# Mixture-of-experts rows that carry their weight, and gathers that add by DMA

## The reference, cut to what matters

```python
x = x + attn_a(layernorm(x))
x = x + ffn(layernorm(x))
x = x + attn_b(layernorm(x))
x = x + ffn(layernorm(x))

def ffn(x):                       # E = 16 experts, K = 2 choices, D = H = 128
    probs = softmax(xf @ router_w)
    w, idx = top_k(probs, K)
    ...                           # rank of each choice in its expert; keep = rank < capacity
    w = where(keep, w, 0.0)
    xe = x_pad[dispatch]          # rows sorted by expert
    hidden = silu(xe @ gate_w) * (xe @ up_w)
    out = (hidden @ down_w) * wbuf[:, :, None]
    combined = zeros.at[dispatch].add(out)
    return combined
```

## Time and profile before

| | us |
|---|---|
| three timed runs, median | 1406.74 |
| lowest and highest | 1403.67 and 1412.88 |
| profiled execution: its span | 1555.5 |
| TensorE busy in it | 1331.6 (86%) |
| VectorE busy | 1056.7 (68%) |
| GpSimd busy | 833.1 (54%) |
| ScalarE busy | 759.3 (49%) |

### The profile page before, as it was taken

One profiled execution on the slowest core, in us unless ns is written; L12 is line 12 of the kernel. 1 busy time (PEld: TensorE's weight loads), 2 busy tenths in 40 slices (PEclk: granted clock), 3 DMA queues, 4 the chain that ended last, 5 costly groups with the idle time before them and its releaser, 6 DMA issues.

```text
span 1555.5 us, 28624 instructions
## 1 busy us (share of the span) xinstructions
PE 1331.6 (86%) x8534; PEld 822.4 (53%) x8534; DVE 1056.7 (68%) x4590; ACT 759.3 (49%) x1901; POOL 833.1 (54%) x1246
## 2 busy tenths in 40 slices
PE   3999998978996989999999999999999999767400
PEld 1566655547885955444444444444455588656400
DVE  2899998883643477888778788787798546433422
ACT  2444444424544666666556566555566455333200
POOL 3247776675323133466666567755555345435576
PEclk9999998987998988999889799887699899988755
DMA  6755312013444410000000000020001134444432
GB/s 171 244 171 188 115 38 69 25 52 111 157 151 135 137 31 15 15 21 28 25 25 28 18 25 28 27 77 23 23 18 42 34 122 153 132 129 138 145 79 73
DMA packets 119785, 125.82 MB, mean 81 GB/s; under 512 B 15568, under 2 KB 109904, under 8 KB 119632
## 3 DMA queue, kind: packets, MB, share of 16 engines
q1 hardware_dynamic: 103248, 90.42, 18.3%
q0 software_dynamic: 16384, 33.59, 7.5%
HBM read 50.15 MB, written 73.79 MB: 80 GB/s over the span
## 4 chain that ended last, share of the span: by engine, by line
PE 68%; DVE 9%; issue 6%; another core or an unknown queue 5%; POOL 5%; ACT 4%; DMA 0%; ACTq 0%; POOLq 0%; DVEq 0%
PE pair L1897 27%; PE pair L1823 8%; PE pair L1834 4%; POOL vmyg L563 4%; PE pair L1685 4%; PE bank L1709 3%; DVE pT L1126 2%; PE pair L1812 2%; PE bank L1630 2%; DVE pT L1401 2%; PE bank L1925 1%; PE bank L1624 1%; PE bank L1951 1%; PE pair L1674 1%
## 5 line engine op out<-in xcount | busy, mean ns | idle before, releaser
L1897 PE MATMUL pair<-kT,apart 32*128 32x512 f32 x2048 | 500.4, 733 | 8.0 <-DVE smax L1401 6.5
L1401 DVE CUSTOM_DVE_ANT_0 pT<-pair,pT 128x256 f32<-128x256 f32 x1024 | 385.4, 417 | 128.5 <-ACT pT L924 110.1
L924 ACT ACTIVATE pT<-pair 128x256 f32<-128x256 f32 x1024 | 327.1, 395 | 257.1 <-PE pair L1897 229.2
L1897 PEld LDWEIGHTS pair<-kT,apart 32*128 32x128 f32 x2048 | 198.5, 208 | 155.4 <-DVE smax L1401 97.8
L563 POOL DMA_INDIRECT vmyg<-ybufA,slg x128 | 123.2, 962 | 149.8 <-DVE smax L1401 67.3
L1293 DVE TENSOR_TENSOR hid<-sg,pair 128x512 f32<-128x512 f32 x96 | 65.9, 686 | 197.6 <-ACT sg L850 171.2
L1823 PE MATMUL pair<-xeT,unit_w 128*128 128x256 f32 x768 | 195.6, 400 | 0.8 <-issue 0.8
L563 POOL DMA_INDIRECT vmyg<-ybufB,slg x128 | 122.7, 958 | 91.9 <-DVE smax L1401 47.6
L1126 DVE TENSOR_TENSOR pT<-pair,causal 128x512 f32<-128x512 f32 x256 | 159.5, 681 | 12.5 <-PE pair L1685 12.3
L1834 PE MATMUL pair<-unit_w,hid 128*128 128x128 f32 x768 | 110.7, 291 | 61.9 <-DVE ye L1301 61.6
L508 POOL DMA_INDIRECT dispB<-xnf,sli x128 | 127.4, 996 | 63.7 <-issue 36.2
(11 more groups left out here) (231 smaller groups left out, 2008.0 us busy)
## 6 DMA issues: line engine op xcount, KB each, us to landing
dispB<-zeros SPq DMA_DIRECT2D x16, 1408.0 KB
apart<-dispA SPq DMA_DIRECT2D x96, 128.0 KB
ybufA<-ye SPq DMA_DIRECT2D x48, 256.0 KB
apart<-dispB SPq DMA_DIRECT2D x96, 128.0 KB
ybufB<-ye SPq DMA_DIRECT2D x48, 256.0 KB
dispA<-zeros SPq DMA_DIRECT2D x33, 128.0 KB
xs<-in_x SPq DMA_DIRECT2D x16, 256.0 KB, 3.2
out<-xs SPq DMA_DIRECT2D x15, 256.0 KB
```

Source lines behind the costliest of these rows:

```text
L924: act.activation(rel[n % RING][:, q, :], pair[n % RING][:, q, HALF:SEQ], ACT.Relu).then_inc(s["relu_done"], 1)
L1401: dve.tensor_tensor_reduce(out=rel[n % RING][:, q, :], in0=pair[n % RING][:, q, 0:HALF], in1=rel[n % RING][:, q, :], scale=1.0, scalar=LOW ...
L1897: pe.matmul(pair[n % RING][:, q, :], apart[h][at, j, t * P:(t + 1) * P], kTs[h][at, HALF:], start=True, stop=True).then_inc(s["bsc_done"], 1)
```

## The change

A row that is sent now has 132 columns (528 bytes; `RW`): the 128 features, the weight in column 128, and three zeros. As a token's two choices have different weights, each tile has a copy for each choice: `rows` holds both, `xnf` is the first of them, and `twin` on ScalarE makes the second. `places` writes the weights there, and `wts` is gone. `y_copy` becomes a product of the result with column 128 of the group's rows, so the rows must stay in their tile until then: `load` of group g + 4 waits for `y_ready` of group g, and stands behind the store of g in SyncE's order. The gathers add straight into `xs` (`compute_op=ALU.add`), all those of a batch's first choice before those of its second; `yg`, `indices` and all of VectorE's additions are gone. Those who waited for the additions wait for the landing of the gathers of the second choice. The gathers that follow expert stages 2 and 3 are issued in two runs of eight batches, the second choice of a batch behind the first choice of the next.

```diff
+RW = D + 4
...
-        dispA = nc.dram_tensor("dispA", [DUMMY + UR, D], F32).ap()
+        dispA = nc.dram_tensor("dispA", [DUMMY + UR, RW], F32).ap()
...
-        xnf = [sb(f"xnf{r}", [P, TB, D]) for r in range(NF)]
+        rows = [sb(f"rows{r}", [P, TB, K, RW]) for r in range(NF)]
+        xnf = [t[:, :, 0, 0:D] for t in rows]
...
-        xe = [[apart[h][:, r, :].rearrange("p (j d) -> p j d", d=D) for r in range(NX)] for h in range(2)]
+        xe = [[turns[h][:, r * GT * RW:(r + 1) * GT * RW].rearrange("p (j d) -> p j d", d=RW) for r in range(NX)] for h in range(2)]
...
             def load(seg, g):
                 r = g % NX
                 if g >= NX:
-                    sp.wait_ge(s["xe_tp"], seg * GRP + g - NX + 1)
+                    sp.wait_ge(s["y_ready"], seg * GRP + g - NX + 2)
...
-                for g in range(GRP - 1):
+                for g in range(GRP - 3):
+                    store(g)
                     if g + NX < GRP:
                         load(seg, g + NX)
-                    if g >= 2:
-                        store(g - 2)
...
                     pool.wait_ge(s["slots_ready"], g + 1)
+                    pool.wait_ge(s["twin"], g + 1)
...
-                            in_=xnf[g % NF][:, j, :], in_offset=None, bounds_check=DUMMY - 1, oob_is_err=False,
+                            in_=rows[g % NF][:, j, k, :], in_offset=None, bounds_check=DUMMY - 1, oob_is_err=False,
...
-                pool.tensor_tensor(wts[:, cols].rearrange("p (t k) -> p t k", k=K), topw[:, :, :], keep[:, :, :], ALU.mult)
+                pool.tensor_tensor(rows[g % NF][:, :, :, D], topw[:, :, :], keep[:, :, :], ALU.mult)
...
+            def fetch(g, k, tiles=range(TB)):
+
+                b = g % B
+                if k == 0 and 0 in tiles:
+
+                    pool.wait_ge(s["tb"], SLOTS_AT[g // HALFB])
                     settle(pool)
+                if k and 0 in tiles:
+
+                    pool.wait_ge(s[f"first{g % 2}"], 16 * TB * (g // 2 + 1))
+                for j in tiles:
+                    at = (b * TB + j) * K + k
+                    done = "got_end" if k and (g, j) == (2 * B - 1, TB - 1) else f"{('first', 'second')[k]}{g % 2}"
                     pool.indirect_dma_start(
+                        out=xs[:, b * TB + j, :], out_offset=None, in_=ybuf[second(g)],
+                        in_offset=bass.IndirectOffsetOnAxis(ap=slots[:, at:at + 1], axis=0), compute_op=ALU.add,
+                    ).then_inc(s[done], 16)
...
-            stored(2)
-            fetch(B, 0)
-            fetch(B + 1, 1)
-            for b in range(2, B):
-                if b == HALFB:
-                    stored(3)
-                fetch(B + b, b % 2, end=range(K * (TB - 1), K * TB) if b == B - 1 else ())
+            for seg in (2, 3):
+                stored(seg)
+                at = B + FIRST[seg]
+                fetch(at, 0)
+                for n in range(1, HALFB):
+                    fetch(at + n, 0)
+                    fetch(at + n - 1, 1)
+                fetch(at + HALFB - 1, 1)
...
+            def twin(n):
+
+                act.wait_ge(s["ffn_xn_ready"], n + 1)
+                act.activation(rows[n % NF][:, :, 1, 0:D], xnf[n % NF], ACT.Copy).then_inc(s["twin"], 1)
...
-                    dve.tensor_copy(ye[h][:, :, :].rearrange("p j d -> p (j d)"), bank[7][:, :]).then_inc(s["y_ready"], 1)
+                    dve.tensor_tensor(ye[h][:, :, :], bank[7].rearrange("p (j d) -> p j d", j=GT),
+                                      xe[seg % 2][g % NX][:, :, D:D + 1].to_broadcast([P, GT, D]), ALU.mult).then_inc(s["y_ready"], 1)
...
-                    if fetch and n in (18, 19):
-                        add_first(b + 2, h, ((0, 1), (2, 3))[n - 18])
-                    if fetch and n in (20, 21):
-                        add_second(b + 2, h, ((0, 1), (2, 3))[n - 20])
                     if fetch and n == 22:
-                        dve.wait_ge(s["combined"], b + 3)
+                        dve.wait_ge(s[f"second{h}"], 16 * TB * (b // 2 + 2))
```

More of the change, by code:

```diff
@@ L190, in build @@
         tails = sb("tails", [1, E], I32)
-        apart = [sb(f"apart{h}", [P, GH, SEQ]) for h in range(2)]
-        whose = sb("whose", [P, NT * K, E])
-        xe = [[apart[h][:, r, :].rearrange("p (j d) -> p j d", d=D) for r in range(NX)] for h in range(2)]
+        turns = [sb(f"turns{h}", [P, NX * GT * RW]) for h in range(2)]
+        apart = [turns[h][:, 0:GH * SEQ].rearrange("p (j t) -> p j t", j=GH) for h in range(2)]
+        whose = sb("whose", [P, HALFB * TB * K, E])
+        xe = [[turns[h][:, r * GT * RW:(r + 1) * GT * RW].rearrange("p (j d) -> p j d", d=RW) for r in range(NX)] for h in range(2)]
         xeT = [sb(f"xeT{h}", [P, GT, D]) for h in range(2)]
@@ L245, in build @@
         block = ctx.enter_context(nc.Block())
+        SLOTS_AT = (28, 34, 51, 68)
         def tiles_of(b):
@@ L463, in _ @@
             pool.memset(ohsum[:, :], 0.0)
-            pool.memset(vmyg[:, :], 0.0).then_inc(s["vm_zero"], 1)
+            for r in range(NF):
+                pool.memset(rows[r][:, :, :, D:RW], 0.0)
+            pool.memset(vm[:, :, :], 0.0).then_inc(s["vm_zero"], 1)
             pool.memset(m8f[:, :], -1.0)
@@ L656, in _ @@
             stored(0)
-            fetch(0, 0)
-            fetch(1, 1)
+            for k in range(K):
+                fetch(0, k)
+                fetch(1, k)
             def selected_rows(b):
@@ L829, in attention_a @@
                     apply_norm(b + 2, b + 2, xna, "att", int(last), b + 2)
+                if last:
+                    twin(b - 1)
             apply_norm(0, 0, xna, "att", 0, 0)
@@ L875, in chain_a @@
                     turned(B - 1, "ffn", xfT)
+                    twin(B - 1)
                 if g == 5:
@@ L946, in body @@
                         context_x(b - 1)
+                    if before and n == 25:
+                        twin(b - 2 + B)
                     if before and n == 26:
@@ L974, in pieces @@
                     turned(2 * B - 2, "ffn", xfT)
+                    twin(2 * B - 2)
                 if g == 5:
@@ L983, in pieces @@
                     turned(2 * B - 1, "ffn", xfT)
+                    twin(2 * B - 1)
                 if g == 14:
@@ L1309, in experts @@
                 y_copy(G - 1)
-            def indices(b, h):
-                dve.tensor_copy(slg[h][:, :], slots[:, bass.ds(b * TB * K, TB * K)]).then_inc(s["slg_ready"], 1)
-            def add_choice(b, h, k, done, tiles=range(TB)):
-                for j in tiles:
-                    xb = xs[:, b * TB + j, :]
-                    last = dve.scalar_tensor_tensor(out=xb, in0=yg[h][:, K * j + k, :],
-                                                    scalar=wts[:, bass.ds((b * TB + j) * K + k, 1)], in1=xb,
-                                                    op0=ALU.mult, op1=ALU.add)
-                if TB - 1 in tiles:
-                    last.then_inc(done, 1)
-            def add_first(b, h, tiles=range(TB)):
-                if 0 in tiles:
-                    dve.wait_ge(s[f"got{h}"], (b // 2 + 1) * 16 * TB * K)
-                add_choice(b, h, 0, s["comb0"], tiles)
-            def add_second(b, h, tiles=range(TB)):
-                if 0 in tiles:
-                    dve.wait_ge(s["comb0"], b + 1)
-                add_choice(b, h, 1, s["combined"], tiles)
             def chain_a(g):
@@ L1370, in chain_a @@
                 if g == 15:
-                    indices(0, 0)
-                    indices(1, 1)
                     dve.wait_ge(s["w_in2"], 16 * 11)
@@ L1466, in body @@
                         residual(b - 2)
-                    if fetch and n == 1:
-                        indices(b + 2, h)
                     if b == MID + 2 and n == 29:
@@ L1811, in turn_x @@
                     for j in range(GT):
-                        last = pe.transpose(bank[2][:, j * P:(j + 1) * P], xe[seg % 2][r][:, j, :], ident[:, :])
+                        last = pe.transpose(bank[2][:, j * P:(j + 1) * P], xe[seg % 2][r][:, j, 0:D], ident[:, :])
                     last.then_inc(s["xe_tp"], 1)
```

80 lines of the change are left out of this document (16 added, 64 removed).

## The result

The changed kernel takes 1642.58 us (median of four runs, 1637.09 to 1654.80) where the kernel before takes 1405.88 beside it: a ratio of 1.1674, with a 95% interval of 1.163 to 1.1719. The sign was forecast, the size was not: 1498 us with a range up to 1555. A ratio leaves out runs that were over 1.5% slower than their kernel's fastest, so it isn't quite the quotient of the two medians.

The account below looks back on a forecast made before the run. It took TensorE to bound attention B and undisturbed expert stages, with gather issue on GpSimd in the tail. Loads +82, clock +12, additions -5, gathers +4, end -2 made +91 on 1406.7: 1498 us, range 1445 to 1555.

Parts of the forecast that it names:

- loads: idleness of TensorE in the stages: Expert stages: tiles refilled only after the result, so late loads stall TensorE; +82 us (60 to 100).
- clock in the stages: Expert stages: TensorE's granted clock falls after idle stretches; +12 us, between nothing and +37.
- attention B: VectorE's additions removed there, 34 us of its work but little of it time; -5 us, between 0 and -34.
- Undisturbed groups: Expert stages: 3.055 us a group at full clock, so four stages take some 310 to 330 us undisturbed.
- faster: Rival: stages at the profiled stage 3's 5.2 us a group, loads nearly in time, only additions count; 1375 us, chance 0.07.
- The loop: Expert stages, transposition to that four groups on: 14.76 us plus stalls against 12.22; stall 1.27 us, group 4.3 us.
- The gathers' price: Tail: a gather that adds by DMA costs 0.06 us more, +4 us; bounds 0 and 0.5 us each (32 us).
- dear gathers: Rival: gathers at 1.75 us each lengthen the tail by 32 us and outlast stage 3; 1537 us, chance 0.2.
- The signs: Timeline: load behind each store, TensorE idle over 1 us per transposition, stores 4.3 us apart, batches about 42, gathers at 1.25.
- Odd rows: Rival: 528-byte rows not starting at multiples of 512 bytes land after 3.2 us; 24 us more, 1522 us, chance 0.07.
- twin: ScalarE, 32 copies of 128x512 at some 0.7 us, needed half a batch later: 0, or 22 us without that cover.
- product: Expert stages, `y_copy`: the product costs what the copy did, 681 ns against 685.

Follow-up runs that it names:

- the two kinds of batch: Changed kernel, attention B gathers in one run, selected_rows behind the normalized rows: 1589.32 us, 1.1278; batches 38.3 us without a wait at pair 23, 48.4 with one.
- the last kernel: Changed kernel with weights kept aside, early loads; GpSimd in attention B: first choices, places, second choices, normalized rows, selected_rows: 1488.42 us, 1.0569.
- the second profile of the kernel before: The kernel before, unchanged, profiled again to get an execution at the pace of the timed runs; it spans 1405.1 us.
- the second padded kernel: The kernel before with a 128x400 addition on GpSimd behind each of the 112 gathers of attention B: 1479.34 us, 1.048.

## Why the prediction was wrong

The two profiles give its terms one by one, by windows of time.

| term | predicted | measured |
|---|---|---|
| loads: idleness of TensorE in the stages | +82 | +90 |
| clock in the stages (with all that makes TensorE's instructions longer) | +12, at most 37 | +42 |
| attention B | -5 | +77 |
| tail behind stage 3 (gathers, and the end) | +4 - 2 | +31 |
| start | 0 | -2 |
| sum | +91 | +238 |

Three steps failed: the price of a gather that adds, put at 0.06 us and measured at 0.6; the wait of a second choice for the first and GpSimd's longer queue in attention B, put at nothing and worth 77 us there; and the clock in the stages, a third of its size.

- **Undisturbed groups** were the right ground. Taking the four stages as 310 to 330 us, from a stretch of 24 us, against the 425 of the profile: measured 330. The rival *faster*, built on the slow stage, was out.
- **The loop** was right, part by part: result to store 0.71 us (0.71 predicted), store to load 1.61 (1.64), landing 2.74 for that load (2.6), landing to TensorE 0.04 (0.1). Short was the way from transposition to result: 13.55 us against 9.71 + 2 x 1.27 = 12.25. Without its stall a group takes 3.27 to 3.54 us there instead of 3.055, and two larger stalls (1.59 and 1.42) lay in it. Hence 4.66 us a group where 4.3 was forecast. The sum took the stall to be the same ahead of each transposition; in the pairs of stage 1 it isn't (5.2 us a group).
- **The clock in the stages** was mis-sized: 0.93 and 0.92 granted. The clock was low for 14 and 16% of them, 69 us, of which at most half, 35 us, is lost work; the rest of the 42 would be groups that no longer overlap. The Trainium skill ("TensorE: Matmul & The Clock Gate", HAM oscillation) tells of a clock that falls in each wait for a load. This trace agrees in part: from 392 to 480 the granted clock stayed at 1.00 through fourteen waits for loads of 0.45 to 2.25 us (a fall came only behind the fifteenth, 2.19 us), and it was 0.83 from 480 to 530, where every second transposition waited 1.9 to 2.6 us. The prediction took +12, a third of its upper end of 37; the 35 us come close to that end, though the clock did not fall in each wait.
- **The gathers' price** is the step that failed outright. "If GpSimd builds it like the plain one, 0"; "I take 0.06 us". No row spoke for 0 rather than for 0.5, and the value was put at the cheap end. Measured +0.6 us, and +74 us for the 128 gathers behind stage 2, beside which the stalls of stage 3 cost nothing more. The rival *dear gathers* had 0.5 us and this overlap, and still came to 1537 only. That its 32 us for the tail are near the 31 of the table is luck: the window of the tail starts where stage 3 ends.
- **Attention B** is what both lacked, and the largest miss. The text names the wait ("a second choice waits for the first of the same batch, issued 5 us earlier") and the queue behind it ("in attention B also the routing work of GpSimd") and puts no price on either. The slack was there to be read: rows ready 4.1 us ahead of TensorE. Measured from the ranks' matmul of a batch (medians of eleven batches), TensorE is free for pair 23 after 22.75 us, 22.76 before: it gained nothing from VectorE's missing additions. On GpSimd the first gather starts 1.4 us earlier, as it no longer waits for the indices; then the first four gathers take 2.4 us more, the fifth starts 2.2 us later behind the fourth, for the landing, the last four take 1.8 us more, and L674 behind them 0.6 (2.18 us; 1.58 before). The rows are 5.6 us later, 1.4 more than the slack, and TensorE waits 1.57 us. By this sum the longer gathers alone, without the 2.2 us for the landing, would just have fitted into the slack. And the 17 us of waits came with 60 us of longer work, as the low clock behind a wait held for some 14 to 20 us: the two kinds of batch show it, and the last kernel, where the wait is gone.
- **The signs.** A load right behind each store, and the DMA into the tile as the releaser of transpositions that wait, came as named; over 1 us of idleness ahead of each transposition (0.45 to 1.71 us in the rows of stage 0, none ahead of every second one in the pairs), 4.3 us a group (4.66, and 5.2 in the pairs of stage 1), 42 us a batch (47.5) and a pitch of 1.25 us (1.85) did not.
- **Odd rows, twin, product**: taken at nothing, and nothing they cost (1.0012).
- Not settled: why the clock also falls without a wait of 0.25 us or more (some 10 us in batches of the last kernels; and in the second profile of the kernel before 34 us of one batch, 1084 to 1121), why it stayed up through the waits from 392 to 480, and what splits the 42 us exactly.

## What to carry to other kernels

Before a queue gets longer work, measure the slack of each thing that it delivers: from the end of the instruction that makes it to the start of the one that takes it. A few us more on an engine that is busy half the time cost nothing until the smallest slack is used up, and then several times themselves, if the waiting engine is TensorE and its clock falls. A new dependence between two items of one queue counts as such work: here the wait for a landing took about as much of the slack as four of the longer gathers. An operation that no trace shows belongs at the middle of its bounds at least, and its price has to be carried through every stage in which it runs, not only the one where it is plainly exposed.

## What the runs showed of the hardware

- An indirect gather of 128 rows that adds into SBUF takes 1.56 us on GpSimd, a plain one 0.96; 144 packets against 32; 256-byte rows take as long as 512-byte ones. It landed 3.2 to 4.0 us after its start (batch at 830).
- In attention B, where TensorE is otherwise busy 98%, its clock fell to 1.2 GHz behind most waits of 0.9 to 2.4 us, and stayed there for 10 to 20 us though TensorE was busy throughout. From 392 to 480, in stages 0 and 1, it stayed up through fourteen waits of up to 2.25 us.
- The instruction on GpSimd right behind an adding gather starts 0.55 us before the gather's recorded end and runs that much longer (L674: 2.18 us for 1.58).
- An addition on GpSimd beside one of VectorE's (128x32, bf16) made that one take 1.27 us for 0.18 (medians of 13, the second padded kernel).
- A profiled execution can be slower than the timed runs that it stands for: 1555.5 us against 1405.1 for the same kernel, some 95 us of it in the expert stages, where a pair of SyncE's load issues took 4.21 us for 0.85, and 57 in attention B.
